# Local attention: both row normalisations on ScalarE with scale and bias, and the sum with the input one step later than them

## The reference, cut to what matters

```python
x = x + _layernorm(_L0_attn_ref(_layernorm(x), w_qkv, w_out))

def _L0_attn_ref(x, w_qkv, w_out):            # H = 16 heads, D = 64
    xn = rms_norm(x)
    q, k, v = split(xn @ w_qkv.T)             # 128 -> 3 * 1024
    q, k = apply_rope(q), apply_rope(k)
    attn = softmax(where(0 <= q_pos - k_pos <= 32, q @ k.T / 8, -1e9))
    return (attn @ v) @ w_out.T

def _layernorm(x, eps=1e-05):                 # over the last axis
    return (x - mean(x)) / sqrt(var(x) + eps)
```

## Time and profile before

| | us |
|---|---|
| median of 3 runs | 2562.07 |
| lowest and highest | 2557.89, 2569.11 |
| the profiled execution, its own time | 2554.34 |
| its span, first to last instruction | 2552.5 |
| local attention within it | about 0 to 992 |

### The profile page before, as it was taken

How to read it: one execution, slowest core, us unless ns; L and a number is a source line. 1 busy time by engine, 2 the same in 40 slices (tenths; PEclk the granted TensorE clock), 3 DMA queues, 4 the chain that set the end, 5 groups by cost and what they waited for, 6 DMA issues and landing times. The chain is left out here.

```text
span 2552.5 us, 68349 instructions
## 1 busy us (share of the span) xinstructions
PE 2029.0 (79%) x26748; PEld 1180.0 (46%) x26748; DVE 1951.9 (76%) x5296; ACT 1552.8 (61%) x2872; POOL 1276.3 (50%) x1115
## 2 busy tenths in 40 slices
PE   5999999999999996311167828899898988988698
PEld 3777777777777776300033312233233322322354
DVE  4777787778777775787746717899999989997586
ACT  4666666666666662000033417788888888887598
POOL 5777777666777771005475267533433343331122
PEclk9999999999999997555588958999999999999799
DMA  4333333333333330001132232321122112210001
GB/s 120 82 84 83 82 81 85 77 77 85 85 77 89 81 81 8 0 0 39 49 96 79 69 68 60 51 41 27 26 34 40 30 26 32 39 33 2 14 27 36
DMA packets 105797, 140.13 MB, mean 55 GB/s; under 512 B 24949, under 2 KB 80149, under 8 KB 105238
## 3 DMA queue, kind: packets, MB, share of 16 engines
q1 hardware_dynamic: 99350, 123.37, 22.0%
q0 software_dynamic: 6144, 12.60, 1.7%
HBM read 26.55 MB, written 16.78 MB: 17 GB/s over the span
## 5 line engine op out<-in xcount | busy, mean ns | idle before, releaser
L1841 DVE TENSOR_REDUCE d_nmax_<-d_s_ 128x2 bf16<-128x1024 f32 x512 | 612.7, 1220 | 75.1 <-PE d_s_ L2003 72.4
L1752 ACT ACTIVATE d_pT_<-d_t_ 128x512 f32<-128x512 f32 x1024 | 558.3, 602 | 118.8 <-PE d_t_ L2015 105.9
L281 POOL TENSOR_TENSOR a_other<-a_other,a_rope 128x512 f32<-128x512 f32 x256 | 325.3, 1292 | 261.3 <-DMA a_other<-a_raw 261.0
L2028 PE MATMUL d_o_<-d_pT_,d_v_ 128*32 128x256 f32 x4096 | 316.9, 393 | 0.2 <-ACT d_pT_ L1752 0.2
L349 ACT ACTIVATE a_pT<-a_t 64x384 f32<-64x384 f32 x512 | 248.1, 485 | 18.8 <-PE a_t L604 7.7
L2015 PE MATMUL d_t_<-d_qs_,d_ks_ 49*128 49x512 bf16 x1024 | 202.2, 390 | 53.7 <-ACT d_pT_ L1752 49.9
L312 ACT COPY a_v<-a_proj 128x512 f32<-128x512 f32 x128 | 74.9, 586 | 238.2 <-PE a_proj L514 238.2
L2003 PE MATMUL d_s_<-d_ks_,d_qs_ 48*128 48x512 bf16 x1024 | 200.8, 387 | 14.8 <-DVE d_nmax_ L1841 9.5
L1208 ACT ACTIVATE c_hT_<-c_in_,c_beta_,c_gamma_ 128x512 f32<-128x512 f32 x16 | 12.4, 777 | 281.6 <-PE c_in_ L1329 281.6
L2015 PEld LDWEIGHTS d_t_<-d_qs_,d_ks_ 49*128 49x128 bf16 x1024 | 50.9, 93 | 279.6 <-ACT d_pT_ L1752 202.4
L2028 PEld LDWEIGHTS d_o_<-d_pT_,d_v_ 128*32 128x32 f32 x4096 | 87.8, 108 | 181.2 <-ACT d_pT_ L1752 121.2
(11 more groups left out here) (267 smaller groups left out, 4827.0 us busy)
## 6 DMA issues: line engine op xcount, KB each, us to landing
a_other<-a_raw SPq DMA_DIRECT2D x512, 128.0 KB, 2.3
d_qs_<-d_part_ SPq DMA_DIRECT2D x192, 64.0 KB
d_ks_<-d_part_ SPq DMA_DIRECT2D x192, 64.0 KB
a_xpre<-x SPq DMA_DIRECT2D x16, 256.0 KB, 3.8
a_xres<-x SPq DMA_DIRECT2D x16, 256.0 KB, 3.8
c_xs_<-sorted_x SPq DMA_DIRECT2D x16, 256.0 KB, 2.7
c_w_<-e_w SPq DMA_DIRECT2D x16, 256.0 KB
sorted_x<-c_xs_ SPq DMA_DIRECT2D x16, 256.0 KB, 2.0
```

What stands on the lines that cost most here:

```text
L281: nc.gpsimd.tensor_tensor(other[s % 2][:, side, :], other[s % 2][:, side, :], rope[:, 1, :], ALU.mult).then_inc(rope2_done, 1)
L1752: nc.scalar.activation(pT[kt][pair][:, a, :], t_bank(j, turn)[:], ACT.Exp).then_inc(t_read, 1)
L1841: nc.vector.reduce_max(out, s_bank(unit, e)[:], AX_X, negate=True).then_inc(s_read, 1)
L2028: ins = nc.tensor.matmul(o_ps[HC * i:HC * (i + 1), cols], v[e.k][:, kt, g * GH + i, :], pT[kt][i // 2][:, i % 2, cols], start=(kt, half) = ...
```

## The change

The normalisation of the input (at NORM_X) and of the output (at OUT_Y) moves from VectorE's queue to ScalarE's. ScalarE computes scale times input plus bias, so the subtraction of the mean becomes a bias of minus mean times factor: VectorE forms minus the mean (`minus1`, `minus2`) with the statistics, and GpSimd multiplies that by the factor right after the power (`shift1`, `shift2`). ScalarE's output normalisation is due at step 16 (OUT_Y is now 16, in the step of ROOT_Y), at the end of its step; VectorE's sum with the input stays at 17 under the name ADD_X.

```diff
-        LOAD_RES, COPY_Y, STAT_Y, ROOT_Y, OUT_Y, SUM_Y, ROOT_SUM = 10, 14, 15, 16, 17, 18, 19
+        LOAD_RES, COPY_Y, STAT_Y, ROOT_Y, OUT_Y, ADD_X, SUM_Y, ROOT_SUM = 10, 14, 15, 16, 16, 17, 18, 19
...
             def factors(b):
                 pool.wait_ge(stats1, b + 1)
                 nc.gpsimd.tensor_tensor(comb[:], ve[:], neg_half[:], ALU.pow).then_inc(comb_ready, 1)
+                pool.wait_ge(comb_ready, b + 1)
+                nc.gpsimd.tensor_tensor(shift1[:], minus1[:], comb[:], ALU.mult).then_inc(shift1_ready, 1)
...
                 if due(s, ROOT_Y, before, left):
-                    pool.wait_ge(stats2, batch_of(b, s, ROOT_Y) + 1)
+                    e = batch_of(b, s, ROOT_Y)
+                    pool.wait_ge(stats2, e + 1)
                     nc.gpsimd.tensor_tensor(rstd2[:], ve2[:], neg_half[:], ALU.pow).then_inc(rstd2_ready, 1)
+                    pool.wait_ge(rstd2_ready, e + 1)
+                    nc.gpsimd.tensor_tensor(shift2[:], minus2[:], rstd2[:], ALU.mult).then_inc(shift2_ready, 1)
...
         def _(act):
+            def normalised(b):
+                act.wait_ge(shift1_ready, b + 1)
+                for t in range(NT):
+                    ins = nc.scalar.activation(xpre[:, t, :], xpre[:, t, :], ACT.Identity, bias=shift1[:, t:t + 1],
+                                               scale=comb[:, t:t + 1])
+                ins.then_inc(xn_ready, 1)
+
+            def output_normalised(b):
+                act.wait_ge(shift2_ready, b + 1)
+                for t in range(NT):
+                    ins = nc.scalar.activation(ysb[:, t, :], ysb[:, t, :], ACT.Identity, bias=shift2[:, t:t + 1],
+                                               scale=rstd2[:, t:t + 1])
+                ins.then_inc(y_normed, 1)
...
             nc.scalar.copy(identb[:], ident[:]).then_inc(identb_ready, 1)
+            normalised(0)
             turned(0, 0, 0, 0)
...
                 if alive(LAG_EXP, before, left):
                     exponentials(n - LAG_EXP, (s - LAG_EXP) % PAIRS)
+                if due(s, NORM_X, before, left):
+                    normalised(batch_of(b, s, NORM_X))
+                if due(s, OUT_Y, before, left):
+                    output_normalised(batch_of(b, s, OUT_Y))
...
                 dve.wait_ge(x_stat, 2 * b + 2)
+                nc.vector.tensor_scalar(minus1[:], mv1[:, :, 0], -1.0, None, ALU.mult)
                 nc.vector.tensor_scalar(ve[:], mv1[:, :, 1], 1.0 + 1e-6, 1e-11, ALU.mult, ALU.add).then_inc(stats1, 1)
-
-            def normalised(b):
-                dve.wait_ge(comb_ready, b + 1)
-                for t in range(NT):
-                    ins = nc.vector.tensor_scalar(xpre[:, t, :], xpre[:, t, :], mv1[:, t, 0:1], comb[:, t:t + 1],
-                                                  ALU.subtract, ALU.mult)
-                ins.then_inc(xn_ready, 1)
...
+                nc.vector.tensor_scalar(minus2[:], mv2[:, :, 0], -1.0, None, ALU.mult)
                 nc.vector.tensor_scalar(ve2[:], mv2[:, :, 1], 1e-5, None, ALU.add).then_inc(stats2, 1)
 
             def output(b):
-                dve.wait_ge(rstd2_ready, b + 1)
-                for t in range(NT):
-                    ins = nc.vector.tensor_scalar(ysb[:, t, :], ysb[:, t, :], mv2[:, t, 0:1],
-                                                  rstd2[:, t:t + 1], ALU.subtract, ALU.mult)
-                ins.then_inc(ynorm_done, 1)
-                dve.wait_ge(ynorm_done, 2 * b + 2)
+                dve.wait_ge(y_normed, b + 1)
                 dve.wait_ge(xres_in, 16 * (b + 1))
                 nc.vector.tensor_tensor(x1[:, bass.ds(NT * b, NT), :], ysb[:], xres[:], ALU.add).then_inc(x1_ready, 1)
...
-                if due(s, NORM_X, before, left):
-                    normalised(batch_of(b, s, NORM_X))
-                if due(s, OUT_Y, before, left):
-                    output(batch_of(b, s, OUT_Y))
+                if due(s, ADD_X, before, left):
+                    output(batch_of(b, s, ADD_X))
```

More of the change, by code:

```diff
@@ L90, in l0_attention @@
         comb = sb("comb", [128, NT])
+        minus1 = sb("minus1", [128, NT])
+        minus2 = sb("minus2", [128, NT])
+        shift1 = sb("shift1", [128, NT])
+        shift2 = sb("shift2", [128, NT])
         st3 = sb("st3", [128, NT, 6])
@@ L112, in l0_attention @@
         comb_ready = sem("comb_ready")
+        shift1_ready = sem("shift1_ready")
+        shift2_ready = sem("shift2_ready")
+        y_normed = sem("y_normed")
         xn_ready = sem("xn_ready")
@@ L402, in _ @@
             statistics(0)
-            normalised(0)
             turned_low(0, 0)
@@ L418, in output_statistics @@
                 ins.then_inc(ynorm_done, 1)
-                dve.wait_ge(ynorm_done, 2 * b + 1)
+                dve.wait_ge(ynorm_done, b + 1)
+                nc.vector.tensor_scalar(minus2[:], mv2[:, :, 0], -1.0, None, ALU.mult)
                 nc.vector.tensor_scalar(ve2[:], mv2[:, :, 1], 1e-5, None, ALU.add).then_inc(stats2, 1)
             def output(b):
-                dve.wait_ge(rstd2_ready, b + 1)
-                for t in range(NT):
-                    ins = nc.vector.tensor_scalar(ysb[:, t, :], ysb[:, t, :], mv2[:, t, 0:1],
-                                                  rstd2[:, t:t + 1], ALU.subtract, ALU.mult)
-                ins.then_inc(ynorm_done, 1)
-                dve.wait_ge(ynorm_done, 2 * b + 2)
+                dve.wait_ge(y_normed, b + 1)
                 dve.wait_ge(xres_in, 16 * (b + 1))
```

## The result

The changed kernel takes 2668.9 us (median of four runs, 2665.3 to 2675.5) against 2560.2 us (four runs): 1.041 times the time before, with a 95% interval of 1.038 to 1.045. It is 109 us slower; the forecast was 2637 us, or 80 us more on the profiled execution, in a range of 2588 to 2680. The profiled execution of the changed kernel is its slowest run, 2675.5 us with a span of 2672.7; that is 121 us more than the profiled execution of the kernel before.

The account below looks back on a forecast made before the run. TensorE was taken to set the pace of the local attention. The terms 91 + 17 + 10 - 28 - 11 + 1 = +80 on 2554.3 gave 2634, plus 3 for scatter 2637 us, range 2588 to 2680.

Parts of the forecast that it names:

- The mechanism: Local attention, step 1: ScalarE waits about 5 us for GpSimd's shift, raw copies follow, TensorE waits about 7 us.
- The output's wait: End of step 16: ScalarE waits for GpSimd's shift, making step 1's raw copy 6.5 us late; 14 x 6.5 = +91.
- The clock: After each batch's pause of nearly 7 us TensorE loses 1.2 to a low clock: 14 x 1.2 = +17.
- The input's normalisation: On ScalarE at the end of step 3, ahead of step 4's raw copy: 0.7 of 1.5 left, fifteen times, +10.
- What is caught up: While ScalarE is held, GpSimd finishes its step and some key casts' waits vanish: 0.8 a batch, -11.
- What is taken away: VectorE's stall at step 2 (20 us), its clock loss (5) and VectorE's spared work (3): -28.
- Head and tail: Ends of the local attention: last normalisation 1.5 instead of 1.1, with a negation and product more, +1; head a wash.
- (a): Rival, faster: GpSimd's power is done when ScalarE finishes step 16; about 2539 us, at best 2520; chance 5%.

Follow-up runs that it names:

- the filled pause: Changed kernel with 36 extra matmuls of no use in TensorE's pause of step 17: 1.031 times the kernel before.
- the power first: Kernel before with only GpSimd's power for the output moved ahead of rope in step 16: 0.991 times the kernel before; repeated, 2534.0 us, 0.990.

## Why the prediction was right, and where it was off

**The mechanism** was right in every part that it named: ScalarE waits for the shift of the same step, the raw copy stands behind it, TensorE has no slack there, and the pause lowers the clock. The experiments that took the wait away gave back 91 to 93 of the 109 us.

**The output's wait** was forecast as 6.5 at step 1 and is 6.7. ScalarE waited 5.2 where 4.6 + 0.2 + 0.1 was expected, and the four activations took 1.65, not 1.49 + 0.1. These are 94 us against 91.

**The clock** was the term most mis-sized: 1.2 us a batch, taken from what the kernel before lost after waits of 3 to 4 us. It is 2.0, as step 2 and the filled pause both show: 28 against 17. The upper bound named was 2.4. The prediction's own rows allowed more than 1.2: they have 4.10 instead of 2.70, and the distance of 8.05 to the next projection is 1.4 over the 6.6 of an odd step that TensorE alone sets. The changed kernel loses more because the clock is low from the first matmul behind the pause (0.50, where the earlier trace rows have 0.62). With this term too small the batches, said to become 63 to 65 us long, became 66.9.

**The input's normalisation** was forecast to cost 0.7 at step 4, against 0.2 that VectorE gave back; step 4 rose by 1.1. In seven batches it was 7.9 or less, which is the 0.8 above 7.1 that the slack leaves. In the other seven it was 8.4 to 9.4, and the timeline of one shows the swap of step 2 landing late (GpSimd's product starts 7.17 behind the raw copy of 156.17, where 6.3 is the mean) and the casts of step 3 waiting for GpSimd, which eats the slack first:

```profile
163.34 2.54 POOL L290 TENSOR_TENSOR a_other<-a_other,a_rope 128x512 f32<-128x512 f32 x2 [2.76 <-DMA a_other<-a_raw]
```

```profile
163.24 1.23 ACT L357 COPY a_raw<-a_proj 128x512 f32<-128x512 f32 x2 [0.32 <-PE a_proj L540]
...
167.20 0.62 ACT L363 CAST a_qB<-a_qT 128x512 bf16<-128x512 f32 x1 [0.66 <-POOL a_qT L295]
168.37 0.62 ACT L365 CAST a_kB<-a_kT 128x512 bf16<-128x512 f32 x1 [0.56 <-POOL a_kT L295]
...
170.93 1.65 ACT L315 ACTIVATE a_xpre<-a_xpre,a_shift,a_comb 128x128 f32<-128x128 f32 x4
172.61 1.07 ACT L357 COPY a_raw<-a_proj 128x512 f32<-128x512 f32 x2
...
174.13 0.47 PE L532 MATMUL a_proj<-a_w_lo,a_xnT_hi 128*128 128x512 f32 x1 [1.85 <-DVE a_qT L477]
```

In three of the seven, this one among them, the granted clock fell behind the wait, here of 1.85 us, and step 5 took 8.9 where 7.3 is even, though the prediction had taken it that waits of 2 us cost no clock:

```profile
174.13:179.00 4.87, 4.87 (x85) 3.64 (x85) 2.99 (x4) 2.90 (x6) 1.50 (x3) 0.65 0.49 111
```

In the fourteen batches step 4 cost some 8 us more than forecast, and in the two ahead of them (9.37 and 8.73 instead of 7.48 and 7.07) 3.6 more.

**What is caught up** was forecast as -11 and is the step that failed. Only step 3 gained, 0.8, of which 0.3 to 0.5 is what the kernel before gained there too when only its stalls were taken away (7.19 and 7.01 in the two runs with the power first, instead of 7.47). Step 5 did not gain, and the key's casts still wait for 25.6 us in total where they waited for 32.7. The waits vanish for two steps, 1 and 2, and come back at step 3. GpSimd's first product follows the raw copy by the same distance in both kernels, 6.0 to 6.5 us in the mean of each step, so what ScalarE gains by being late is lost with the next raw copy.

**What is taken away** came out as said in size: VectorE's stall at step 2 went. Its cause was only half right in the forecast, which took the normalisations beside GpSimd for the fault and VectorE's relief for the cure. The kernel with the power first shows that the order of one GpSimd instruction brought them there.

**Head and tail.** The head is the wash that was expected: ScalarE waits 2.6 us for its first shift, yet the value projection of step 0 in the first batch starts at 22.77 instead of 22.55. Between the profiled executions the last raw copy moves by 113 us; the other 8 of the 121 lie behind it, where the forecast had 1. About half of them are routing's (279 instead of 276 us), which no change of this kernel touches.

Of the rivals, the sign change (a) needed the shift to be there in time. Once an experiment made it so, its figure of 2539 was missed (2576). By the steps four things made the difference, some 7 to 10 us each: 1.65 ahead of step 17's raw copy cost 1.5 and not 1.0, step 2 kept 0.5 of its stall (7.60), step 4 rose by 1.0, and nothing was caught up. The place within the step had to change as well, and then the kernel did come below the one before, by 24 us.

## What to carry to other kernels

Before work is moved to another engine, ask three things of the queue that takes it: is the operand there when that queue arrives (here 5.2 us short), what stands behind the instruction, and where in the step the queue already waits. The same activations cost 109 us behind a wait and 16 to 19 without it; where ScalarE idles anyway the kernel came out 24 us below the one before. That is no gain of the move: all three figures hold the stall that the move takes away, and without the move one instruction's place takes it away too. Against the kernel before with the power first, the three are about 133, 40 to 43, and 0. And look first for a small producer at the end of a queue: moving one power of 128x4 ahead of rope's work gave all that the move to ScalarE gave at its best here. Last, compare the stage that was changed and not only the total: an untouched stage varied by over 10 us between kernels and hid about half of what the input's part cost.

## What was not expected of the hardware

- TensorE's pause of 7.8 us cost 2.0 us more in the work behind it, at a granted clock of 0.50, the 1.2 GHz level, in the stretch shown above (4.80 instead of 2.70); a pause of 5.6 us cost 1.9. Filling the pause with 36 matmuls of no use (6.0 us) kept the mean clock at 1.00 and made the changed kernel faster by 26 us.
- The clock also fell (0.65 over the 4.87 us from 174.13) behind a wait of 1.85 us, while it stayed at 1.00 over the 7.9 us from 262.90 in the kernel before, behind a wait of 1.88. What made the difference is not shown.
- Four activations of 128x128 in place in SBUF take 1.65 us, where four from PSUM take 1.49.
- In four batches of sixteen a wait of 1 us or less was enough to make four 128x128 VectorE operations take 3 to 4 us instead of 1.1: it moved them next to GpSimd's products. The Trainium skill ("SBUF — State Buffer", Who interferes with whom) says that VectorE operations of this kind can, in some modes, need a pair of ports that GpSimd uses too, and that the second to start is then held up for the whole of the other's instruction. The means of 501 and 355 ns fit that; which mode ours run in, no run here shows.
